# Centred output weights, and a spread of reciprocal sums issued from two queues, in a transformer block on one core

## The reference

```python
x = x + layernorm(attention(layernorm(x)))
x = x + layernorm(ffn(layernorm(x)))
# layernorm(t) = (t - mean(t)) / sqrt(var(t) + 1e-5), over the 256 features
# attention: 16 heads of 16 features, rotary positions, causal softmax,
#            then out @ proj_w.T + proj_b
# ffn(x) = (gelu((x @ U1) @ V1 + b1) @ U2) @ V2 + b2,  rank 64, width 1024
```

## Time and profile before

| | us |
|---|---|
| median of 3 runs | 1206.66 |
| lowest, highest | 1205.65, 1210.28 |
| the profiled execution | 1208.03 |
| its span, first to last instruction | 1206.3 |

### The profile page before, as it was taken

How to read it: one execution, slowest core, us unless ns; L and a number is a source line. 1 busy time by engine, 2 the same in 40 slices (tenths; PEclk the granted TensorE clock), 3 DMA queues, 4 the chain that set the end, 5 groups by cost and what they waited for, 6 DMA issues and landing times.

```text
span 1206.3 us, 25813 instructions
## 1 busy us (share of the span) xinstructions
PE 1155.2 (96%) x9844; PEld 619.4 (51%) x9844; DVE 941.1 (78%) x1458; ACT 941.8 (78%) x1898; POOL 658.8 (55%) x718
## 2 busy tenths in 40 slices
PE   5899999999999999999999999999999999999995
PEld 4655446544654456445654564455545554454542
DVE  6998786789678886888678958896888886476666
ACT  4477878788868877887878877887788689678785
POOL 2467325944495349633874387346844343336647
PEclk9899999999999999999999999999999999999998
DMA  6586544665555745576367636762766443402413
GB/s 202 180 143 127 106 66 79 159 130 103 111 140 132 133 81 142 128 107 140 93 147 104 144 81 152 115 151 37 177 117 127 100 96 114 131 1 92 154 54 122
DMA packets 99259, 142.22 MB, mean 118 GB/s; under 512 B 24896, under 2 KB 60992, under 8 KB 99136
## 3 DMA queue, kind: packets, MB, share of 16 engines
q1 hardware_dynamic: 99136, 140.58, 51.9%
HBM read 79.70 MB, written 51.38 MB: 109 GB/s over the span
## 4 chain that ended last, share of the span: by engine, by line
PE 63%; DMA 9%; SPq 8%; DVE 8%; POOL 7%; ACT 3%; issue 2%; DVEq 0%; POOLq 0%; ACTq 0%
PE PV L875 16%; PE RING L857 12%; PE RING L822 10%; PE RING L776 6%; DMA QK<-split_parts 4%; PE RING L886 3%; PE RING L789 3%; PE RING L927 3%; SPq L649 3%; PE RING L920 3%; SPq L624 2%; DVE MB L1015 2%; PE RING L828 2%; DMA X<-x 2%; ACT PB L1206 2%
## 5 line engine op out<-in xcount | busy, mean ns | idle before, releaser
L1206 ACT ACTIVATE PB<-RING 128x512 f32<-128x512 f32 (+2 forms) x1280 | 623.5, 566 | 139.4 <-PE RING L857 130.9
L1015 DVE TENSOR_REDUCE MB<-RING 128x2 f32<-128x1024 f32 (+2 forms) x448 | 497.0, 1142 | 96.1 <-PE RING L828 48.1
L857 PE MATMUL RING<-QK 64*128 64x512 f32 (+3 forms) x1536 | 320.5, 395 | 1.5 <-DMA QK<-NSROW 0.9
L1301 POOL TENSOR_SCALAR_AFFINE_SELECT PB<-PB 128x512 f32<-128x512 f32 x256 | 160.9, 638 | 275.1 <-ACT PB L1206 274.7
L822 PE MATMUL RING<-QK 62*128 62x512 f32 (+3 forms) x1536 | 296.2, 387 | 14.2 <-DMA QK<-split_parts 8.7
L857 PEld LDWEIGHTS RING<-QK 64*128 64x128 f32 x1536 | 169.2, 186 | 156.1 <-ACT PB L1206 92.3
L1015 DVE TENSOR_REDUCE M<-RING 128x2 f32<-128x768 f32 (+1 forms) x186 | 191.3, 1041 | 56.1 <-PE RING L828 55.3
L875 PE MATMUL PV<-PB,VL 128*32 128x512 f32 (+3 forms) x2048 | 224.1, 522 | 0.5
L822 PEld LDWEIGHTS RING<-QK 62*128 62x128 f32 x1536 | 156.7, 186 | 126.8 <-DVE MB L1015 36.3
L828 PE MATMUL RING<-MASKK,MASKQ 64*128 64x128 bf16 (+1 forms) x768 | 112.5, 248 | 0.0
L1231 ACT ACTIVATE F_H<-RING,F_B 128x512 f32<-128x512 f32 x128 | 80.5, 687 | 18.6 <-PE RING L920 18.5
(11 more groups left out here) (141 smaller groups left out, 1507.8 us busy)
## 6 DMA issues: line engine op xcount, KB each, us to landing
QK<-split_parts SPq DMA_DIRECT2D x372, 128.0 KB, 5.8
split_parts<-PARTS SPq DMA_DIRECT2D x60, 256.0 KB, 3.1
split_parts<-EO SPq DMA_DIRECT2D x60, 256.0 KB, 3.6
ATT<-OT SPq DMA_DIRECT2D x128, 64.0 KB
INV<-inverse_sums SPq DMA_DIRECT2D x32, 256.0 KB
block_mid<-Y SPq DMA_DIRECT2D x16, 512.0 KB, 4.4
F_X<-block_mid SPq DMA_DIRECT2D x16, 512.0 KB, 5.6
out<-F_Y SPq DMA_DIRECT2D x32, 256.0 KB, 2.1
```

Of the source, the lines that this page charges most:

```text
L857: ins = e.matmul(m[:, i, :], QK[g % 3][r, 1, k, 128 * j:128 * j + 128], QK[g % 3][r, 0, k, 512 * c + off:512 * c + 512], start=True, stop= ...
L1015: e.tensor_reduce(acc, ring(("max", g, s, u), pairs, n), AX.X, ALU.max).then_inc(v_max, 1)
L1206: e.activation(buf[:, h, pairs[0]:pairs[-1] + 1, :], strip(("score", g, s, u), pairs, n), ACT.Exp).then_inc(a_exp, 1)
L1301: e.affine_select(buf[:, :, 0:128], buf[:, :, 0:128], pattern=[[0, 4], [1, 128]], base=0, channel_multiplier=-1, compare_op=ALU.is_ge, fil ...
```

## The change

1. **Centred weights.** A new step of VectorE, `centre`, subtracts from WP its mean over the 256 output features, row by row, and from BP its mean; `f_centre` does so for V2 and B2. The rows that are projected have mean zero then. The first projection and its copy wait for it.
2. **The norm of the projected rows.** `y_rows` on ScalarE (64 instructions) is gone. `y_scale` on GpSimd multiplies two row tiles at a time (32 instructions). The shift YNM and its two small steps in `y_pow` are gone.
3. **The norm in the feed-forward part.** `f_norm` on ScalarE (60 instructions) is gone. `f_res` on GpSimd multiplies and then adds (row block 0 of parts 0 to 6 and one step of part 7), and on VectorE does both in one instruction for each row tile (17 steps of two). The shift is gone here too.
4. **The second transfer of each spread** is issued by ScalarE (`att_spread_second`, 16 times), with the same waits.
5. **Order and banks.** All five strings of `ORDERS` and `PLACES` are written anew. TensorE's steps are the same but for the two `heat` matmuls, which are gone.

```diff
+def res_by(i, js, a):
+
+    return "POOL" if (a == 0 if i < NB - 1 else (js, a) == (HALVES[0], 1)) else "DVE"
...
-                    for k in range(2):
-                        src = inverse[c, 8 * k:8 * k + 8, :].unsqueeze(1).broadcast_to([8, 16, 512])
-                        e.dma_start(INV[:, k, :], src).then_inc(s_spread, 16)
+                    src = inverse[c, 0:8, :].unsqueeze(1).broadcast_to([8, 16, 512])
+                    e.dma_start(INV[:, 0, :], src).then_inc(s_spread, 16)
                 elif what == "store":
                     b, c = at
...
                     w.wait_ge(g_att, NTH["att_scale", b, c, 1])
+                    w.wait_ge(v_cen, 6)
                     if q % 2 == 0:
...
+                    w.wait_ge(o_mi["fold"], 1)
+                    e.tensor_reduce(MEAN[:, 0:2], WP[:, :, :], AX.X, ALU.add).then_inc(v_cen, 1)
+                    e.tensor_reduce(MEAN[:, 2:3], BP[:, :], AX.X, ALU.add).then_inc(v_cen, 1)
+                    w.wait_ge(v_cen, 2)
+                    e.tensor_scalar(MEAN[:, 0:3], MEAN[:, 0:3], -1.0 / D, None, ALU.mult).then_inc(v_cen, 1)
+                    w.wait_ge(v_cen, 3)
+                    for k in range(2):
+                        e.tensor_scalar(WP[:, k, :], WP[:, k, :], MEAN[:, k:k + 1], None, ALU.add).then_inc(v_cen, 1)
+                    e.tensor_scalar(BP[:, :], BP[:, :], MEAN[:, 2:3], None, ALU.add).then_inc(v_cen, 1)
+                elif what == "f_centre":
+                    w.wait_ge(f_w, 144)
+                    for t, n in (V2, 0), (B2, 1):
+                        e.tensor_reduce(FMEAN[:, n:n + 1], t[:, :], AX.X, ALU.add).then_inc(f_cen, 1)
+                    w.wait_ge(f_cen, 2)
+                    e.tensor_scalar(FMEAN[:, :], FMEAN[:, :], -1.0 / D, None, ALU.mult).then_inc(f_cen, 1)
+                    w.wait_ge(f_cen, 3)
+                    for t, n in (V2, 0), (B2, 1):
+                        e.tensor_scalar(t[:, :], t[:, :], FMEAN[:, n:n + 1], None, ALU.add).then_inc(f_cen, 1)
                 elif what == "att_inverse":
                     b, c = at
...
                     y = FY[i % 2]
-                    rows = slice(js[0], js[-1] + 1)
-                    w.wait_ge(f_yna, NTH["f_norm", i, js, a])
-                    e.tensor_tensor(y[:, a, rows, :], y[:, a, rows, :], X1[i % 5][:, a, rows, :], ALU.add).then_inc(f_resv, 1)
+                    w.wait_ge(f_ypow, NTH["f_spread", i, js])
+                    for j in js:
+                        r = 4 * a + j
+                        ins = e.scalar_tensor_tensor(y[:, a, j, :], y[:, a, j, :], YF[i % 2][3][:, r:r + 1], X1[i % 5][:, a, j, :],
+                                                     ALU.mult, ALU.add)
+                    ins.then_inc(f_resv, 1)
 
 
         def scalar(e):
...
-                elif what == "y_rows":
-                    b, c, j = at
-                    w.wait_ge(g_ynm, NTH["y_dev", b, c])
-                    e.activation(YS[c][:, j, :], YS[c][:, j, :], ACT.Identity,
-                                 scale=YRS[c][:, j:j + 1], bias=YNM[c][:, j:j + 1]).then_inc(a_yn, 1)
+                elif what == "att_spread_second":
+                    b, c = at
+                    w.wait_ge(s_inv[c], 16 * (b + 1))
+                    if b or c:
+                        w.wait_ge(g_att, NTH["att_spread", b, c] * 2 - 2)
+                    src = inverse[c, 8:16, :].unsqueeze(1).broadcast_to([8, 16, 512])
+                    e.dma_start(INV[:, 1, :], src).then_inc(s_spread, 16)
                 elif what == "f_turn_out":
                     n, k = at
                     w.wait_ge(f_t, 2 * n + k + 1)
...
                     if b:
-                        w.wait_ge(a_yn, NTH["y_rows", b - 1, c, 3])
+                        w.wait_ge(g_ysc, NTH["y_scale", b - 1, c, 2])
                     e.tensor_scalar(YVE[c][:, :], YMV[c][:, :, 1], EPS, None, ALU.add).then_inc(g_yve, 1)
-                    e.tensor_scalar(YNM[c][:, :], YMV[c][:, :, 0], -1.0, None, ALU.mult).then_inc(g_yve, 1)
-                    w.wait_ge(g_yve, 2 * NTH["y_dev", b, c])
+                    w.wait_ge(g_yve, NTH["y_dev", b, c])
                     e.tensor_tensor(YRS[c][:, :], YVE[c][:, :], HALF[:, 0:4], ALU.pow).then_inc(g_yrs, 1)
+                elif what == "y_scale":
+                    b, c, j0 = at
                     w.wait_ge(g_yrs, NTH["y_dev", b, c])
-                    e.tensor_tensor(YNM[c][:, :], YNM[c][:, :], YRS[c][:, :], ALU.mult).then_inc(g_ynm, 1)
+                    scale = YRS[c][:, j0:j0 + 2].unsqueeze(2).to_broadcast([128, 2, D])
+                    e.tensor_tensor(YS[c][:, j0:j0 + 2, :], YS[c][:, j0:j0 + 2, :], scale, ALU.mult).then_inc(g_ysc, 1)
                 elif what == "residual":
                     b, c, j0 = at
-                    w.wait_ge(a_yn, NTH["y_rows", b, c, 3])
+                    w.wait_ge(g_ysc, NTH["y_scale", b, c, j0])
                     e.tensor_tensor(YS[c][:, j0:j0 + 2, :], YS[c][:, j0:j0 + 2, :], X[b % 3][:, 4 * c + j0:4 * c + j0 + 2, :],
...
-                    w.wait_ge(f_ypow, NTH["f_spread", i, js])
-                    e.tensor_tensor(yn, yn, yr, ALU.mult).then_inc(f_ynm, 1)
                 elif what == "f_res":
                     i, js, a = at
-                    y = FY[i % 2]
-                    rows = slice(js[0], js[-1] + 1)
-                    w.wait_ge(f_yn if (i, a) == (NB - 1, 1) else f_yna, NTH["f_norm", i, js, a])
+                    y, rows = FY[i % 2], slice(js[0], js[-1] + 1)
+                    w.wait_ge(f_ypow, NTH["f_spread", i, js])
+                    scale = YF[i % 2][3][:, 4 * a + js[0]:4 * a + js[-1] + 1].unsqueeze(2).to_broadcast([128, 2, D])
+                    e.tensor_tensor(y[:, a, rows, :], y[:, a, rows, :], scale, ALU.mult).then_inc(f_ysc, 1)
+                    w.wait_ge(f_ysc, NTH[step])
                     e.tensor_tensor(y[:, a, rows, :], y[:, a, rows, :], X1[i % 5][:, a, rows, :], ALU.add).then_inc(f_res, 1)
```

Of the tables only the first row of one, as a sample:

```diff
 ORDERS = {
     "PE": (
-        "HxxqqqqqqqqvvvvxxfqqqqqqqvqvvvxmmxmmmmqvFqqvhhmmqmmmqqmssqmssmqmsmsmvmvmsmxptmsmmsmxmssmpsmpmsssmsspssmsmq"
...
+        "HxxqqqqqqqvqvvvxxfqqqqqvqqqvvvxxmmmmmmqqFvqvmmqmmqqmmssqmmssqmmsvmsmvmmsxptmsmxsmsmmpmspmsssmsssmspmmsqssm"
```

More of the change, by code:

```diff
@@ L130, in taken_by @@
         return engine == rope_by(*at[:3])
-    if what in ("f_norm", "f_res"):
-        last = at[0] == NB - 1 and at[2] == int(what == "f_norm")
-        return (engine == "DVE") == last
-    return True
+    if what == "f_res":
+        return engine == res_by(*at)
+    return True
+def res_by(i, js, a):
+    return "POOL" if (a == 0 if i < NB - 1 else (js, a) == (HALVES[0], 1)) else "DVE"
 LETTERS = {
@@ L383, in block_kernel @@
             YRS = [sb(f"YRS{i}", [128, 4]) for i in range(2)]
-            YNM = [sb(f"YNM{i}", [128, 4]) for i in range(2)]
+            MEAN = sb("MEAN", [128, 4])
         def sb(name, shape, dt=fp32):
@@ L732, in sync @@
                     i, = at
-                    w.wait_ge(f_res, max(NTH["f_res", i - 5, js, a] for js in HALVES for a in range(2)))
+                    for a in range(2):
+                        w.wait_ge(f_resv if a else f_res, max(NTH["f_res", i - 5, js, a] for js in HALVES))
                     load_f(i)
@@ L736, in sync @@
                     i, js, a = at
[L737 removed]
+                    w.wait_ge(f_resv if res_by(i, js, a) == "DVE" else f_res, NTH["f_res", i, js, a])
                     rows = slice(js[0], js[-1] + 1)
```

244 lines of the change are left out of this document (114 added, 130 removed).

## The result

The changed kernel takes **1218.04 us** (median, 1216.82 to 1223.18) against 1206.66: ratio 1.0104, 95% interval 1.0057 to 1.0151. It is slower by 11.4 us where 15.3 us less were forecast; the time lies outside the range. The profiled execution is the longest of the three, 1223.18 us with a span of 1221.5.

The account below looks back on a forecast made before the run. It took three engines sharing PSUM banks to bound the attention, none full on average, with half of ScalarE's relief passing. -12 + 1 - 2 - 2.3 = -15.3 us gave 1192.7 profiled, 1191.4 us as median; range 1177 to 1206, some 80%.

Parts of the forecast that it names:

- ScalarE in the attention: Attention: norms off ScalarE less added DMA issues leave it 23.9 us less work; half was taken to pass, -12 us.
- At one end nothing: Attention, low end of ScalarE's term: none of its relief reaches the end, as VectorE is 83 to 89% busy there.
- the feed-forward part: Behind the attention: ScalarE loses 60 norms, VectorE gains 34 fused multiply-adds at 0.41 us; -2 us, from -8 to +5.
- The port lock: Rival, feed-forward part: VectorE's fused steps wait for GpSimd's wide steps over shared ports; 1196 to 1198 us, 4%.
- Centring: VectorE before the first projection: centring WP and BP takes 2.3 us, half of which passes; +1 us.
- GpSimd in the attention: Attention: 28 multiplications at 1282 ns fall where GpSimd is 40 to 49% busy; 0 us, from 0 to +18.
- The masks: Rival, attention: GpSimd's multiplications delay masks and each holds a product 0.64 us; +18 us, 1209.4 us, 7%.
- the rewriting: The whole order written anew: helps to spend the room, but no row prices it, so nothing by itself.
- SyncE: Spread transfers: SyncE issues 16 fewer, 10.3 us, and second halves can start 0.64 us earlier; 0 us.
- slower rival: Attention: ScalarE waits at its DMA issues for reciprocals to land, stopping exponentials and TensorE; 1219 us, 11%.
- The end: Behind the last matmuls: four fused steps replace norms and additions, shift dropped; -2.3 us, from -3 to 0.

Follow-up runs that it names:

- no_rows: The kernel before, with all 64 ScalarE norms of the projected rows left out and nothing put in their place: ratio 1.0012.
- g_wide_out: The changed kernel with GpSimd's multiplications and additions of the first seven feed-forward samples cut to 8 of 256 columns, VectorE's steps kept: ratio 1.0060.
- lock_alone: Separate small kernel timing VectorE's steps with GpSimd idle, then beside its 128x512 additions: eight fused steps took 3.3 us, then 11.2 us.
- both_out: The changed kernel with VectorE's fused and GpSimd's wide steps of the first seven feed-forward samples cut to 8 of 256 columns: ratio 1.0008.
- order_bare: As both_out, also without the centring of WP and BP and GpSimd's multiplications in the attention, both spread transfers issued by SyncE: ratio 0.9980.
- steps_old_order: The kernel before in its old order, with centring added and GpSimd's multiplications replacing ScalarE's row norms in batches 0 to 6: ratio 1.0108.
- att_only: The changed kernel's steps and order up to the last score, the kernel before's feed-forward part behind it: ratio 1.0064.
- spread_sp: The changed kernel with both transfers of every spread issued by SyncE again: ratio 1.0104.
- fused_end: The kernel before with V2 and B2 centred and only the last sample's rows closed as in the changed kernel: ratio 0.9981.

## Why the prediction was wrong

- **The failed step** is "ScalarE in the attention", -12 us. It set aside that TensorE showed work in 917 of 930 us and read the 115.7 us in which weight loads waited for exponentials as time that a loaded ScalarE costs. no_rows takes all 32.9 us away and gains nothing (1.0012), with the same waits. "At one end nothing" was the right end. The reason given there, VectorE, isn't borne out by its waits, which didn't grow (26.0 + 13.6 us against 47.2), but no run took work off it. What paces the stage in ScalarE's place stays open.
- **Mis-sized: the feed-forward part**, -2 us with +5 as its worst; it was +10.8. The count of 34 steps held; at 0.41 us each they are 14 us, and they took 14.6 in g_wide_out but 27.2 beside GpSimd's wide steps. The port lock was among the rivals at 4% and +5 to +7 us. The size of its waiting was right (11 us said, 12.6 measured), but it was placed in VectorE's idle time, and idle time elsewhere doesn't help: a fused pair or a row norm late by one GpSimd step stands ahead of the copy that TensorE's next turn needs. The Trainium skill ("SBUF — State Buffer", SBUF: two separate sides) states this lock. lock_alone agrees and adds the price: 1.0 us on each step, at 8 columns as at 256. Lock and length together explain the part's loss, since both_out has none; with the lock gone from the fused steps in g_wide_out some 4 us of it are left, which are the new steps' own length, and the term had put them in VectorE's idle time too.
- **Centring**, +1 us, and **GpSimd in the attention**, 0 us: with the issue they cost about 3.4 us together (both_out against order_bare). The centring took 4 us on VectorE, not 2.3, its shift of three columns slowed as such shifts are in lock_alone (162 ns alone, 682 beside GpSimd). GpSimd's multiplication was cheaper than its price in the sum, 1040 ns and not 1282; one of its inputs is two numbers per partition, and that this is the reason isn't shown.
- **The masks** (rival, 7%): true for the old order (+10.8 us in steps_old_order), mostly hidden by the new one. The prediction put the rewriting at nothing; it is worth some 5 to 10 us here (by the ratios, steps_old_order's 1.08% against att_only's 0.64%, or against the 0.28% that the steps cost in the new order), all of it spent on covering the new steps.
- **SyncE**, 0, and the **slower rival** of ScalarE standing in front of the landing: the issue took 0.60 us (0.644 assumed), ScalarE waited 0.3 us there in all, spread_sp is like the changed kernel. That the time came out near this rival's 1219 us is chance.
- **The end**, -2.3 us: 0.7 in the changed kernel, 1.7 in fused_end, 2.4 where GpSimd's or VectorE's steps of sample 6 are cut. So the full term came only with work left out. In the changed kernel a pair of fused steps of sample 6 beside GpSimd's multiplication is in the way of the last sample's first copy:

```profile
1206.18 2.66 DVE L1154 SCALAR_TENSOR_TENSOR F_Y<-F_Y,F_YRS,F_X 128x256 f32<-128x256 f32 x2 [0.93 <-POOL F_YRS L1358]
...
1208.77 0.68 DVE L1129 TENSOR_TENSOR F_Y<-PV,F_B 128x512 f32<-128x512 f32 x1
```

By the ratios the loss divides in three: from both_out to the changed kernel 0.96% or 11.6 us, the feed-forward part's steps (1.7 us of it at the end, by the traces); from order_bare to both_out 0.28% or 3.4 us, the attention's steps; and order_bare itself -0.20% or -2.4 us, the new order, the new end and the work it leaves out. That these add up to the measured 12.6 us, 1.04%, is no check, as each starts where the last one ends.

## What to carry to other kernels

A wait of TensorE's weight loads for an engine doesn't show that engine as the bound. Where the engine's own idle time behind TensorE is as large (125.0 us here) and it has 3% of the chain that ended last, taking work off it may give nothing; leaving the work out in a trial kernel settles it before a rewrite. Before two engines get work side by side, count how many of VectorE's steps read SBUF in the locking forms, price each at up to a whole step of GpSimd's (1.0 us more beside additions of 1.29 us here), and see what is queued behind them. A step moved to an engine with idle time is free only in an order that covers it.
